# Fourth edge stage of a graph network: ten edge groups fetched row by row from two queues, and all one-hots of the selected groups made by VectorE

## What is computed

```python
h = x @ W
norm = dinv[src] * dinv[dst]
agg = segment_sum(h[src] * norm[:, None], dst, N)      # over all edges
```

## Time and profile before

| | us |
|---|---|
| three runs | 11138.41, 11160.38, 11165.17 |
| median | 11160.38 |
| profiled execution, its own time | 11197.17 |
| its span in the trace | 11195.4 |
| in it, the edge stage (first indirect DMA of L1873 to the last addition) | 8679 to 11134 |

### The profile page before, as it was taken

One profiled execution on the slowest core, in us unless ns is written; L12 is line 12 of the kernel. 1 busy time (PEld: TensorE's weight loads), 2 busy tenths in 40 slices (PEclk: granted clock), 3 DMA queues, 4 the chain that ended last, 5 costly groups with the idle time before them and its releaser, 6 DMA issues. The chain is left out here.

```text
span 11195.4 us, 158258 instructions
## 1 busy us (share of the span) xinstructions
PE 7512.2 (67%) x45679; PEld 5676.2 (51%) x45679; DVE 6853.5 (61%) x18737; ACT 4365.1 (39%) x7367; POOL 7061.2 (63%) x6167
## 2 busy tenths in 40 slices
PE   1333333335899998998956777777777677777775
PEld 1322322333666666666645666666666344444443
DVE  3555555566677777666655666666666444444445
ACT  1111121121667776666621111111111566666664
POOL 3666666662688888888855555556554655555554
PEclk5555555556889999999977888888888788888887
DMA  4434434442666666777761111111111111111111
GB/s 118 110 96 105 111 98 104 101 97 65 103 106 106 107 106 109 109 109 109 110 117 46 43 43 43 43 42 43 42 42 46 45 43 44 44 44 45 44 44 43
DMA packets 1068830, 846.48 MB, mean 76 GB/s; under 512 B 404136, under 2 KB 907183, under 8 KB 1067542
## 3 DMA queue, kind: packets, MB, share of 16 engines
q0 software_dynamic: 360512, 407.88, 20.9%
q1 hardware_dynamic: 676812, 313.54, 12.7%
q10 hardware_dynamic: 30652, 115.04, 3.1%
HBM read 696.14 MB, written 139.60 MB: 75 GB/s over the span
## 5 line engine op out<-in xcount | busy, mean ns | idle before, releaser
L1474 POOL DMA_INDIRECT sums<-sumrows,index x1460 | 2458.1, 1684 | 694.3 <-issue 348.9
L1623 POOL DMA_INDIRECT rows<-table,index x1612 | 1583.8, 982 | 1128.8 <-DVE mid L1680 582.1
L679 POOL DMA_INDIRECT rows<-table,index x1612 | 1609.3, 998 | 1015.9 <-issue 692.0
L1873 POOL DMA_INDIRECT ACC<-table,index x1472 | 1398.4, 950 | 1129.2 <-DVEq L1998 615.1
L1650 DVE TENSOR_TENSOR ACC<-ACC,psS 128x256 f32 x1612 | 674.6, 418 | 792.1 <-PE psS L1714 471.2
L1714 PEld LDWEIGHTS psS<-hot,mid 128*128 128x128 f32 x6448 | 1042.9, 230 | 57.7 <-issue 3.0
L1714 PE MATMUL psS<-hot,mid 128*128 128x128 f32 x6448 | 1032.2, 313 | 2.7 <-DVE mid L1680 2.3
L2045 PE MATMUL psG<-limbs,pickA 128*128 128x384 bf16 x4060 | 902.1, 355 | 159.4 <-issue 102.7
L1910 ACT ACTIVATE pickA<-apart,K 128x512 bf16<-128x512 bf16 x1015 | 721.2, 711 | 717.2 <-remote 475.0
L1966 DVE TENSOR_TENSOR pickD<-ACC,psK 128x512 bf16<-128x512 f32 x700 | 459.9, 682 | 746.4 <-remote 545.4
L1421 PE MATMUL psB<-pickD,limbs 128*128 128x512 bf16 (+1 forms) x2964 | 824.5, 391 | 81.5 <-DVE pickD L1288 77.0
(11 more groups left out here) (349 smaller groups left out, 15303.0 us busy)
## 6 DMA issues: line engine op xcount, KB each, us to landing
win<-table SPq DMA_DIRECT2D x1612, 64.5 KB
srow<-src_f SPq DMA_DIRECT2D x365, 256.0 KB
HN<-rel_f ACTq DMA_DIRECT2D x102, 512.0 KB
relB<-rel_f ACTq DMA_DIRECT2D x102, 512.0 KB
rows<-table,index POOLq DMA_INDIRECT x3224
er<-limbs SPq DMA_DIRECT2D x1632, 3.0 KB
ACC<-table,index POOLq DMA_INDIRECT x1472
sums<-sumrows,index POOLq DMA_INDIRECT x1460
```

The costliest lines, as they stand in the source:

```text
L679: nc.gpsimd.indirect_dma_start(out=rows[:, r, k, :], out_offset=None, in_=table0[:, :], in_offset=bass.IndirectOffsetOnAxis(ap=index[:, n ...
L1474: nc.gpsimd.indirect_dma_start(out=sums1[u][:, :], in_=sums[:, n % 2, u, :], in_offset=None, compute_op=ALU.add, out_offset=bass.IndirectO ...
L1623: nc.gpsimd.indirect_dma_start(out=rows[:, n % R, u, :], out_offset=None, in_=table2[:, :], in_offset=bass.IndirectOffsetOnAxis(ap=index[: ...
L1873: nc.gpsimd.indirect_dma_start(out=rows[:, n % R, u, :], out_offset=None, in_=table3[:, :], in_offset=bass.IndirectOffsetOnAxis(ap=index[: ...
```

## The change

1. Ten front groups are no longer fetched by POOL. Groups 82, 152, 222, 292 and 362 (`BYSP`) are fetched by SP, and 80, 150, 220, 290 and 360 (`BYACT`) by ACT, one 512-byte row per DMA, 512 DMAs per group. The row's address is a register: eight source numbers at a time are loaded into registers (`eight`) from a list of 256 in SBUF, which is itself fetched twice per group. A group's 64 batches of eight are spread over seven back groups (`STEPS = 7`), so that in each back group's ten iterations SP and ACT issue nine or ten batches each. The rows land in two buffers in `SRC`; before a buffer is filled again, the issuing engine waits for the sums of its last group.
2. POOL fetches the 358 others (`QUICK`), through the same ring of four.
3. All 49 one-hots of a back group are made by DVE, with one comparison (`tensor_scalar`) of 16-bit integers (`short`, made by one ACT copy per back group, `shorten`) with a per-partition number in SBUF, into one ring `pick` of nine. ACT's `distance` and `pick` are gone, as are `pickA` and `pickD`.
4. ACT's order is now, for each back group: `gate` (first seven), its row DMAs (`some(m)`), `leave(m)`, `shorten(m + 2)`. SP's `names` DMA stands between two parts of its row DMAs.

```diff
-                RING, BANKS = 4, 3
+                RING, BANKS = 9, 3
+                BYSP = [82 + 70 * k for k in range(5)]
+                BYACT = [80 + 70 * k for k in range(5)]
+                QUICK = [n for n in range(FRONT) if n not in BYSP + BYACT]
+                PACE = 8
...
+                STEPS, BATCH = 7, U * P // PACE
...
+                def eight(eng, numbers, i):
+                    _, at = nc.values_load_multi_w_load_instructions(
+                        numbers[0:1, i % 256:i % 256 + PACE], engines=(eng.engine,), min_val=0, max_val=NPAD - 1,
...
-                        for n in range(FRONT):
-                            pool.wait_ge(s_done, n + 1)
+                        for f, n in enumerate(QUICK):
+                            pool.wait_ge(s_done, QUICK[f - R] + R + 1 if f >= R else 1)
...
+                        def shorten(m):
+                            act.wait_ge(s_names[m % 2], 16 * (m // 2) + 16)
+                            if m > 1:
+                                act.wait_ge(s_pick, TN * (m - 1))
+                            nc.scalar.copy(short[:, m % 2, :], names[:, m % 2, :]).then_inc(s_short, 1)
...
+                        def some(m):
+                            k, step = divmod(m, STEPS)
+                            for b in range(BATCH * step // STEPS, BATCH * (step + 1) // STEPS):
+                                if b == 0 and k:
+                                    act.wait_ge(s_sum, turn_of(BYACT[k - 1]) + 1)
+                                if b % (BATCH // 2) == 0:
+                                    half = b // (BATCH // 2)
+                                    act.dma_start(listC.rearrange("o (t p) -> o t p", t=2), numbers_of(BYACT[k], half), allow_slow_non_contiguous=True).then_inc(s_listC, 16)
+                                    act.wait_ge(s_listC, 32 * k + 16 * half + 16)
+                                at = eight(act, listC, b * PACE)
+                                for i in range(PACE):
+                                    u, p = divmod(b * PACE + i, P)
+                                    act.dma_start(rowsC[p:p + 1, u, :], table3[bass.ds(at[i], 1), :]).then_inc(s_rowsC[u], 16)
...
                         for m in range(BACK):
...
                             if m < steps:
                                 gate(m)
-                        leave(BACK - 1)
+                            some(m)
+                            leave(m)
+                            if m + 2 < BACK:
+                                shorten(m + 2)
...
                             for b in own:
-                                if b in onD:
...
+                                at = m * TN + b
+                                if b == 0:
+                                    dve.wait_ge(s_short, m + 1)
+                                if at >= RING:
+                                    dve.wait_ge(s_used, at - RING + 1)
+                                nc.vector.tensor_scalar(pick[:, at % RING, :], short[:, m % 2, :], nodes[:, b:b + 1], None, ALU.is_equal).then_inc(s_pick, 1)
```

More of the change, by code:

```diff
@@ L1803, in build @@
                 lows = sb("lows3", [P, TN])
[L1804 to L1806 removed]
+                short = sb("short3", [P, 2, U * P], mybir.dt.int16)
+                nodes = sb("nodes3", [P, TN])
+                pick = sb("pick3", [P, RING, U * P], BF16)
                 rowsL = sb("rowsL3", [P, U, 3 * C], BF16)
@@ L1847, in tiles, with numbers_of @@
                     return slice(g * TG, (g + 1) * TG)
+                def numbers_of(n, half):
+                    return a["src_cols"][:, n * U + 2 * half:n * U + 2 * half + 2].rearrange("p t -> t p").unsqueeze(0)
+                def eight(eng, numbers, i):
+                    _, at = nc.values_load_multi_w_load_instructions(
+                        numbers[0:1, i % 256:i % 256 + PACE], engines=(eng.engine,), min_val=0, max_val=NPAD - 1,
+                        skip_runtime_bounds_check_because="a src is a node number, and padding edges have one too")
+                    return at
                 with nc.Block() as block:
@@ L1851, in _, with some @@
                     def _(sp):
+                        def some(m, which):
+                            k, step = divmod(m, STEPS)
+                            for b in list(range(BATCH * step // STEPS, BATCH * (step + 1) // STEPS))[which.start:which.stop]:
+                                if b == 0 and k:
+                                    sp.wait_ge(s_sum, turn_of(BYSP[k - 1]) + 1)
+                                if b % (BATCH // 2) == 0:
+                                    half = b // (BATCH // 2)
+                                    sp.dma_start(listP.rearrange("o (t p) -> o t p", t=2), numbers_of(BYSP[k], half), allow_slow_non_contiguous=True).then_inc(s_listP, 16)
+                                    sp.wait_ge(s_listP, 32 * k + 16 * half + 16)
+                                at = eight(sp, listP, b * PACE)
+                                for i in range(PACE):
+                                    u, p = divmod(b * PACE + i, P)
+                                    sp.dma_start(rowsP[p:p + 1, u, :], table3[bass.ds(at[i], 1), :]).then_inc(s_rowsP[u], 16)
                         sp.dma_start(index[:, :], a["src_cols"]).then_inc(s_index, 16)
@@ L2012, in sums @@
                         def sums(n):
-                            r, turn = n % R, turn_of(n)
+                            turn = turn_of(n)
                             pe.wait_ge(s_hot, n + 1)
-                            pe.wait_ge(s_rows[r], 16 * U * (n // R) + 16 * U)
+                            if n in BYSP:
+                                chosen = rowsP
+                                for u in range(U):
+                                    pe.wait_ge(s_rowsP[u], 16 * P * (BYSP.index(n) + 1))
+                            elif n in BYACT:
+                                chosen = rowsC
+                                for u in range(U):
+                                    pe.wait_ge(s_rowsC[u], 16 * P * (BYACT.index(n) + 1))
+                            else:
+                                f = QUICK.index(n)
+                                chosen = rows[:, f % R, :, :]
+                                pe.wait_ge(s_rows[f % R], 16 * U * (f // R) + 16 * U)
                             pe.wait_ge(s_free, turn * U + U)
                             for u in range(U):
-                                done = nc.tensor.matmul(psS[:, turn % BANKS, u * P:(u + 1) * P], rows[:, r, u, :], hot[:, n % 2, u, :], start=True, stop=True)
+                                done = nc.tensor.matmul(psS[:, turn % BANKS, u * P:(u + 1) * P], chosen[:, u, :], hot[:, n % 2, u, :], start=True, stop=True)
                             done.then_inc(s_sum, 1)
@@ L2035, in gather @@
                                 pe.wait_ge(s_lo, b // TG + 1)
[L2036 to L2043, removed]
+                            at = m * TN + b
+                            pe.wait_ge(s_pick, at + 1)
+                            chosen = pick[:, at % RING, :]
                             for u in range(U):
                                 done = nc.tensor.matmul(psG[:, u, 0:3 * C], chosen[:, u * P:(u + 1) * P], limbs[:, b, :], start=b == 0, stop=b == TN - 1)
-                            done.then_inc(used, 1)
+                            done.then_inc(s_used, 1)
                         for i in range(FRONT):
```

70 lines of the change are left out of this document (28 added, 42 removed).

## The result

The changed kernel takes 11317.2 us (median of 4 runs, 11306.7 to 11326.1); the kernel before, run beside it, 11162.8 (median of 4). The ratio is 1.0141, 95% interval 1.0121 to 1.0161: slower by 154 us, where 40 us faster was forecast. The profiled execution took 11306.7 us with a span of 11304.7.

The account below looks back on a forecast made before the run. No engine is full: the 2455 us stage is POOL's running time (1840) plus pauses waiting for DVE's `add` (615). Ten groups fewer, -50, and POOL's stretch, +10, give -40: 11160 to 11120 us, range 10980 to 11290.

Parts of the forecast that it names:

- The row DMAs: Last stage, SP and ACT: 73 row DMAs per back group on each, covered by the time of ten iterations; cost 0.
- theory D: From the experiments, last stage: all engines' instructions draw on one allowance in a POOL run, then get one slot per 0.70 us.
- POOL, ten groups fewer, -50: Last stage, POOL: 10 x 4 DMAs of 1.25 us less running time, pauses unchanged; gain 50 us.
- ACT's picks 0: Last stage, ACT: 1015 pairs of activations go, but PE waited for them only 55 us; taken as 0, bound -55.
- DVE's picks 0: Last stage, DVE: 700 comparisons at 0.682 us become 1715 at 0.348, covered within ten iterations; cost 0.
- POOL stretch +10: Last stage, POOL: faster DVE comparisons stretch each of 1432 DMAs by 0.007 us; +10 us, bounds 0 and 200.
- The Trainium skill's rule: Last stage: two-port VectorE instructions lock POOL out of a shared port; rival with chance 0.06, slower, 11450.
- The rows in time: Last stage: at about 0.47 us per SP DMA, group 80 is ready at the latest at i = 77; PE asks at 80.
- `add` comes one block later: Rival, chance 0.18, slower: with the ring of nine, `add` waits for a block of its own iteration; 182 us less 50, 11292.
- ACT or the row DMAs are too slow: Rival, chance 0.09, slower: at 0.9 us per DMA `leave` is late by 8 us in 35 back groups; 290 us, 11400.
- The range: Whole kernel, 8 in 10: 10980 (a quarter of the way to POOL's floor) to 11290 (later `add`, nothing recovered).

Follow-up runs that it names:

- the picks alone: Changed kernel with both row-fetch lists empty, so POOL fetches all 368 front groups and no row DMAs are issued: 11167.9 us, ratio 0.9995 to the kernel before.
- the rows left out: Changed kernel without the 5120 row DMAs, their lists and register loads, POOL still fetching 358 groups: 11132.7 us, ratio 0.9965 to the kernel before.
- constant rows: Changed kernel with the 5120 row DMAs issued for constant rows, without register loads or register instructions: 11194.7 us, ratio 1.0027 to the kernel before.
- five groups: Changed kernel with only SP's five groups fetched row by row, ACT's five back on POOL: 11235.4 us, ratio 1.0074 to the kernel before.
- the picks alone and `add` first: Changed kernel without row DMAs, all 368 groups on POOL, `add` and `s_done` ahead of the next picks: 9469.7 and 9491.7 us, ratios 0.9999 and 0.9997.

## Why the prediction was wrong

**The step that failed** is "*The row DMAs.* ... Cost 0". It cost 185 us in the runs (205 in the profiled stage). I priced the DMAs in the time of ACT and SP alone, against `leave` and the asking of groups 80 and 82, and there the cover held for `leave` in 34 of 35 back groups. I didn't price them in what the prediction itself had found to set the cycle: the time after POOL's resumption in which PE is fast. By the count, that time is not PE's alone. Counted in the traces (all engines' records from POOL's resumption to the first 2.5 us with at most three PE records per half microsecond, medians over the stage), all engines together start 177 instructions before the stretch begins in before, 180 with the picks alone, 178 with the rows left out, 170 with constant rows, 166 with five groups, and 170 in the changed kernel. The middle eight tenths are wide, 149 to 196 in before and 118 to 184 in the changed kernel, but the medians hardly move. PE's mean share of them does: 120, 122, 118, 111, 97 and 89. The 43 records of SP and ACT in the changed kernel stand where PE's stood. So PE finishes two groups in a run of POOL and not three, while each pause stays near 4.7 us in the median. POOL's pauses over 0.8 us sum to 859 us in place of 645 with the rows left out: 214 us, the 205 of the stage. Two smaller parts of it are delays that the row DMAs cause directly: the one late `leave`, whose pause is 12 us longer than the median one, and PE's four waits for late rows, 41 us, of which not all need be lost.

What is shown: the row DMAs, with the register instructions and loads that belong to them, are the cause, the picks and the ring are not; the loss goes with the instructions fetched and not with the number of transfers; PE's slow stretch begins earlier. Within the slow stretches PE is no slower for them: 1.65 records per us in before, 1.64 in the changed kernel, where SP and ACT add 3.6. So theory D's second half, slots taken from PE in these stretches, falls; the stretches begin earlier.

What is argued, not shown: that all engines' instructions share one allowance. One pair of runs speaks against a plain count of them: the kernel before has 31245 records in the stage and the picks alone 29220. At the 11.5 ns per record that the row DMAs cost (185 us for 16037), the 2025 fewer should give 23 us; measured is 0.6, with an interval from 20 us faster to 8 slower. A register-addressed DMA that is dearer in itself than one of a constant row would also fit the 62 and 185 us, and with five groups the loss per DMA (33 ns against 36) fits either. Instructions without any DMA, which would have told them apart, never met the condition. The Trainium skill (NOTIFIC — the notification-queue block, "7.1 Overflow: three behaviours, one of which stalls the engine") says that the block that writes the records of instructions holds its producers back, rather than lose a record, when its internal queues fill. An allowance counted in instructions of all engines, and 0.70 us for an instruction of whatever kind after it, would fit that, but no run here shows such a hold. Every timed run here has a span and a clock from such records, so no run could show what the kernels take without them, and part of the 154 us may belong to the recording.

**The other steps.**

- *POOL, ten groups fewer, -50.* Right in size: -49.6 in the profiled stage, -35 in the runs; -42.5 where POOL is the bound.
- *ACT's picks 0, DVE's picks 0.* Right for both together, 0.9995; they weren't parted. A pick took 0.377 us in the mean, not 0.348.
- *POOL stretch +10.* Measured 0: mean 950 ns beside 1715 picks. What stretches the second stage's scatter stays unknown; the rows didn't show that it is DVE, as the prediction had it. The Trainium skill's rule (SBUF — State Buffer, "SBUF: two separate sides"), by which the picks would have blocked POOL, had 11450; in this case the trace doesn't show the blocking.
- *The rows in time.* Wrong in part. A DMA with its two register instructions has medians of 225 + 37 + 29 ns on SP, less than the 0.47 us I took. But the 1.88 us of the earlier trace rows were a good case (the next four of that line took 2.23 us), and in the stage 2560 of them were spread over 2589 us, one per 1.0 us (waits included), and PE found four groups late. Without slow stretches SP issued 191 in 100 us.
- *The rival "`add` comes one block later"* had the right sign and nearly the size (11292), by a mechanism that isn't there: with a ring of ten it took 11323.6, and with a ring of nine and no row DMAs 11167.9.
- *The rival "ACT or the row DMAs are too slow"* named small DMAs that keep PE slow in a half sentence, but its price hung on a `leave` that is late in all 35 back groups; it was late in one.
- *The range.* A quarter of the way to POOL's floor is 10995, as in the rival's own sum, not the 10980 of the range.

The model of the stage itself (POOL's running time plus pauses that PE's work requires) held in every run; what was missing is what else shortens the fast time.

## What to carry to other kernels

When an engine slows down for reasons that the trace calls "issue", count the instructions of every engine around it, not only its own: work moved to idle queues as thousands of small instructions was not free here (185 us). Price an offload in the resource that sets the cycle, not only in the time of the engine that takes it. And measure a change that removes load from a queue beside the kernel before more than once at different times: here the sign depended on whether POOL ever paused.

## What the runs showed of the hardware that was not expected

- The same kernel takes 11168 us in one condition and 9464 to 9495 in another, and one chip showed both. In the second the last stage has no pause of POOL, PE has no slow stretch (its weight loads for `psG` idle 0.7 us by "issue" with the picks alone and `add` first, in place of 481.1 with the picks alone), and the granted clock in the stage is 0.97 and not 0.82. Between the two profiles of the changed kernel the stage is 799 us shorter, and the untouched stages ahead of it 1048 us (it starts at 7584 in place of 8632). The traces don't show what sets the condition.
- In the slow stretches SP's instructions go in steps of about 0.70 us, a register move (697 and 702 ns) like a DMA (700 and 707).
- 5120 single-row DMAs beside POOL's gathers don't slow the gathers: mean 950 ns in one condition, with them and without, and 955 with against 950 without in the other.
- 5120 DMAs of constant rows cost 62 us; the same number with register addresses 185.
